# A two-direction state-space mixer with routed experts: one input multiply in three steps moved from GpSimd to VectorE

## The reference, cut to what matters

```
h = layernorm(x) * (1 + ca) + sa                  # x: 2 x 2048 tokens x 256
xn = layernorm(h, ln_w, ln_b)
# for each direction (forward, and on the reversed sequence), d = 0..511, n = 0..15:
xp, z = split(xn @ W_in.T)
xc = silu(causal_conv4(xp) + b_conv)
dt, B, C = split(xc @ W_x.T)
dt = softplus(dt @ W_dt.T + b_dt)
state[d, n] = state[d, n] * exp(dt[d] * A[d, n]) + (dt[d] * xc[d]) * B[n]   # token after token
y[d] = sum_n state[d, n] * C[n] + xc[d] * D[d]
out += 0.5 * (y * silu(z)) @ W_out.T
# then a layernorm, top-2 of 8 experts per token, and a shared expert
```

## Time and profile before

| | |
|---|---|
| median of 3 runs | 2154.33 us (2154.12 to 2154.85) |
| the profiled execution, its own time | 2153.5 us |
| its span in the trace | 2151.8 us |
| steps 1 to 15, from the start of step 1 to 1672 us | 1490 us |
| one step with states fed in | 98.3 to 100.5 us |
| granted clock of TensorE over the span (1 is 2.4 GHz) | 0.915 |

### The profile page before, as it was taken

The page is one execution under the profiler, slowest core; times in us unless marked ns, Lnnn a source line. Parts: engine busy times, 40 slices in busy tenths (PEclk is TensorE's granted clock), DMA queues, the critical chain, the costliest instruction groups (busy, mean ns, idle before and its releaser), DMA issues.

```text
span 2151.8 us, 26056 instructions
## 1 busy us (share of the span) xinstructions
PE 1872.8 (87%) x6376; PEld 794.9 (37%) x6377; DVE 1956.5 (91%) x1814; ACT 1523.8 (71%) x3148; POOL 1807.5 (84%) x624
## 2 busy tenths in 40 slices
PE   7889898988989898989898888889775799999997
PEld 3323232323333332323232323333221466655554
DVE  7989999999999999999999999999999776556776
ACT  5876879798888879786878888887956333434443
POOL 5689999999999999999999999999999333415444
PEclk9988898989889898989898998989876899999999
DMA  7746445353625354453535263545434652335444
GB/s 261 248 111 155 105 124 123 101 127 102 156 74 145 97 142 109 122 124 110 127 102 142 77 156 89 135 112 126 102 98 135 235 187 79 109 80 80 78 78 70
DMA packets 140347, 265.32 MB, mean 123 GB/s; under 512 B 21264, under 2 KB 44048, under 8 KB 139072
## 3 DMA queue, kind: packets, MB, share of 16 engines
q1 hardware_dynamic: 125488, 242.05, 41.7%
q0 software_dynamic: 13440, 17.93, 5.0%
q10 hardware_dynamic: 1296, 3.93, 0.5%
HBM read 194.51 MB, written 70.39 MB: 123 GB/s over the span
## 4 chain that ended last, share of the span: by engine, by line
POOL 28%; PE 26%; issue 16%; ACT 15%; DVE 10%; DVEq 2%; DMA 2%; POOLq 0%; SPq 0%; ACTq 0%
POOL hst L940 20%; POOL dbu L928 6%; ACT psum L1257 6%; DVE hst L1611 5%; PE psum L2188 5%; PE psum L2031 4%; PE psum L2200 3%; PE psum L2251 2%; POOL dt L920 2%; PE psum L1951 2%; PE psum L1979 2%; PE psum L1963 1%; DVE dbu L1590 1%; ACT dbu L1289 1%; PE psum L2271 1%
## 5 line engine op out<-in xcount | busy, mean ns | idle before, releaser
L940 POOL TENSOR_TENSOR hst<-hst,c_rep 128x2048 f32<-128x2048 f32 x254 | 1145.6, 4539 | 4.3 <-ACT state L1243 4.3
L1611 DVE TENSOR_TENSOR_SCAN hst<-psum,state,dbu 128x1024 f32<-128x1024 f32 x384 | 878.9, 2330 | 6.1 <-ACT psum L1257 5.5
L1257 ACT ACTIVATE psum<-dt_rep,neg_a 128x512 f32<-128x512 f32 (+1 forms) x1024 | 659.8, 676 | 135.1 <-DVE hst L1611 131.0
L1590 DVE TENSOR_TENSOR dbu<-psum,b_rep 128x2048 f32<-128x2048 f32 x176 | 398.7, 2265 | 8.4 <-PE psum L2016 8.0
L928 POOL TENSOR_TENSOR dbu<-dtu_rep,b_rep 128x2048 f32<-128x2048 f32 x80 | 363.9, 4549 | 8.3 <-DMA dtu_rep<-dtu_scratch 5.6
L2031 PE MATMUL psum<-hst,same 128*32 128x512 f32 x2048 | 285.1, 707 | 82.6 <-POOL hst L940 76.3
L1611 DVE TENSOR_TENSOR_SCAN hst<-psum,dbu 128x1024 f32<-128x1024 f32 x128 | 285.8, 2271 | 13.5 <-ACT psum L1257 12.9
L2016 PE MATMUL psum<-dt,same 32*128 32x512 f32 x352 | 215.6, 694 | 88.8 <-DVE dbu L1590 83.5
L1963 PE MATMUL psum<-xp,taps 128*128 128x512 f32 x512 | 236.6, 605 | 6.6 <-ACT sp_tmp L1226 6.5
L1050 POOL DMA_INDIRECT out_x<-h,target_u x72 | 112.3, 1560 | 153.0 <-DMA out_x<-h,target_u 78.4
L2031 PEld LDWEIGHTS psum<-hst,same 128*32 128x32 f32 x2048 | 68.2, 127 | 307.5 <-issue 172.0
(11 more groups left out here) (186 smaller groups left out, 2516.2 us busy)
## 6 DMA issues: line engine op xcount, KB each, us to landing
dt_rep<-dt_scratch SPq DMA_DIRECT2D x256, 256.0 KB, 4.8
dtu_rep<-dtu_scratch SPq DMA_DIRECT2D x320, 64.0 KB, 1.9
taps<-taps_scratch SPq DMA_DIRECT2D x64, 256.0 KB, 4.6
b_rep<-bc_scratch SPq DMA_DIRECT2D x64, 256.0 KB, 5.0
c_rep<-bc_scratch SPq DMA_DIRECT2D x64, 256.0 KB, 7.8
dt_scratch<-dt SPq DMA_DIRECT2D x63, 256.0 KB, 5.9
h<-slot_scratch SPq DMA_DIRECT2D x72, 129.5 KB
sp_tmp<-t_scratch SPq DMA_DIRECT2D x16, 512.0 KB, 7.0
```

The lines of the kernel that those rows point to most:

```text
L940: nc.gpsimd.tensor_tensor(h, h, c_rep[q % 2][:], ALU.mult).then_inc(prod_done, 1)
L1257: nc.scalar.activation(psum[:, PS_A + i, kept], dt_rep[:, G % 2, j, kept], ACT.Exp, scale=neg_a[:, q % 2, u, i:i + 1]).then_inc(exp_done, 1)
L1590: nc.vector.tensor_tensor(dbu[:, U % DBU, :, :], psum[:, PS_U:PS_U + 1, :].broadcast_to((P, NG, TB)), b_rep[U // UNITS % 2][:], ALU.mult). ...
L1611: nc.vector.tensor_tensor_scan(both(hst[:, U % RING, groups, :]), both(psum[:, PS_A + 2 * pair:PS_A + 2 * pair + 2, :]), both(dbu[:, U % D ...
```

## The change

It takes unit 7 of steps 1, 8 and 9 off GpSimd and gives it to VectorE. The functions that ask who multiplies a unit, or count the multiplies of each engine, follow from `on_pool`. SyncE no longer stores and reads back that unit's rows in these steps. TensorE gets one `spread_input(7)` more in each of them, put ahead of `sum_chunk` at T = 5.

```diff
+LIGHT_STEPS = (1, 8, 9)
...
 def on_pool(U):
-    return U % UNITS in POOL_UNITS
+    return U % UNITS in POOL_UNITS and (U // UNITS not in LIGHT_STEPS or U % UNITS != 7)
...
 def pool_mults(U):
-    return len(POOL_UNITS) * (U // UNITS) + sum(u <= U % UNITS for u in POOL_UNITS)
+    return sum(on_pool(u) for u in range(U + 1))
...
             for q in range(STEPS):
...
-                spread_dtu(q, 7)
+                if on_pool(UNITS * q + 7):
+                    spread_dtu(q, 7)
...
                 if t == 8 or (t == 13 and ahead) or T == 5:
                     spread_input(T + 3)
+                if q in LIGHT_STEPS and t == 5:
+                    spread_input(T + 2)
                 if T == 5:
                     project_dt(0, 3)
                 if t % GN == 1 and T > GN:
                     sum_chunk(T // GN - 1)
-                if 0 < T < ALL_UNITS - 2 and not on_pool(T + 2) and T != 6 and t != 9 and t != 14:
+                if 0 < T < ALL_UNITS - 2 and not on_pool(T + 2) and T != 6 and t not in (5, 9, 14):
                     spread_input(T + 2)
```

## The result

The changed kernel took **2161.03 us** in the median of 8 runs (2158.89 to 2164.21), the kernel before 2154.34 in the median of 8 beside it (2153.54 to 2155.5). The two medians differ by 6.7 us; the ratio on record is 1.0034 (7.3 us), with a 95% interval of 1.0025 to 1.0043: 5 to 9 us slower. The prediction said 2154.8 us and no difference; its range ended at 2159.0. The median misses the range by 2 us, and the kernel is slower where 0.77 of the chance was on "the same".

What follows compares the result with a forecast made beforehand. GpSimd's sum of work was taken as the bound; its shifts of +0.8, -0.8 and +0.5 us summed to +0.5 on an execution of 2153.5 us, 2154.0. With the median 0.8 above, the forecast was 2154.8 us, range 2151.0 to 2159.0.

Steps and rivals of the forecast that it cites:

- The bound: GpSimd's sum of work sets the mixer's end; time follows GpSimd's shift, as long as it doesn't go idle later on.
- What is taken away: Three GpSimd multiplies of 4.5 us, 13.5 us in all; the stores and loads that go with them cost nothing.
- What VectorE pays: Three added multiplies on VectorE, 2.2 us from start to start each, 6.6 us; GpSimd loses nothing by it.
- The new path: At unit 5, step 8: multiply of unit 6, spread, product, sum, z 1, copy, kept state, then GpSimd's weighing: 8.6 us.
- Weighing of unit 5 can start at M + 8.6: GpSimd's start on unit 5 in step 8, before at M + 9.4: 0.8 of 4.5 us kept, 3.7 us idle.
- M: End of VectorE's multiply of unit 6 in a light step, from which the new path is counted; 914.88 in step 8.
- it waits for VectorE's multiply: TensorE's added spread, 1.06 us per step, waits for the multiply of unit 6, with sum and z 1 queued behind.
- Step by step: GpSimd's shift after steps 1, 8 and 9: +0.8, 0.0 and +0.5 us; VectorE's waits give way.
- 13 us of new idle time on GpSimd and 0.5 us too late: What the forecast said becomes of the three steps' gain of 13.5 us.
- The slower one: Rival: the multiply for unit 10 becomes the new wait; about 2161 us if VectorE's waits don't give way; chance 0.15.
- the one on the port: Rival: the added VectorE multiplies block GpSimd, 2.2 us each and 7 in all: 2161 us; chance 0.02.
- The faster one: Rival: the kept state doesn't decide, GpSimd is held by the scan of unit 6 alone; about 2149 us; chance 0.11.

Runs made afterwards that it cites:

- vector_twice: Kernel before, with VectorE's multiply of unit 8 done twice in steps 1, 8 and 9 and nothing else: 2157.03 us, ratio 1.0007.
- fill2: Changed kernel plus two extra overwritten products with diag_d on TensorE ahead of the spread of unit 7 in the three steps: 2155.38 us, ratio 1.0001.
- product_z1_first: Changed kernel with the product with diag_d, then z 1, ahead of the spread of unit 7 on TensorE: 2149.43 us, ratio 0.9978 to the kernel before.
- wait_only: Kernel before, with TensorE waiting ahead of the sum for VectorE's multiply of unit 6 in steps 1, 8 and 9, nothing moved: 2158.34 us, ratio 1.0014.
- save_first: Changed kernel with the kept state of unit 5 ahead of the copy of z 1 on ScalarE in the three steps: 2160.59 us, ratio 1.0026.
- spread_after_sum: Changed kernel with the spread of unit 7 behind the sum and ahead of z 1 on TensorE: 2152.03 us, ratio 0.9991.
- step8_only: Changed kernel with the move in step 8 alone: 2156.88 us, ratio 1.0009 to the kernel before.
- z1_first: Changed kernel with z 1 alone projected ahead of the spread of unit 7 in the three steps: 2155.31 us, ratio 1.0001.
- product_first: Changed kernel with the product with diag_d alone ahead of the spread of unit 7 on TensorE: 2155.7 us, ratio 1.0005, runs 2153.29 to 2161.03.

## Why the prediction was wrong

**The bound: right.** The time follows GpSimd's work plus its idle time. Step 7 is unchanged, and between 175 and 1690 us the only idle times are the three that were named, ahead of the weighing of unit 5.

**What is taken away, 13.5 us: right.** No load became late: no wait of GpSimd for a DMA from 175 us on.

**What VectorE pays, 2.2 us per step: right**, and so was it that waits give way for it (in two of three steps of vector_twice). The multiplies took 2263 ns in the mean over all of after, as in the earlier trace rows. That the added work does not slow GpSimd is as predicted: GpSimd's weighings took 4548 ns in the mean against 4539.

**The new path: the mechanism right, the size wrong.** "Weighing of unit 5 can start at M + 8.6" is the step that failed. It starts at 930.89 with M = 919.39, M + 11.5, in step 8, and at M + 12.0 in step 1. The terms for the spread (1.06, measured 2.07), for the product (1.06, measured 2.01) and for the sum (3.57, measured 4.50) were mis-sized, 2.9 us together; the other terms are off by under 0.1. Each was read from the earlier trace rows, where the clock was 1.00 behind a wait of 1.68 us. The change itself makes another wait there. In the prediction "it waits for VectorE's multiply" is a place in the queue, never a length: from the end of the spread of unit 6 at about 912.6 and M = 914.88 its length would have come out at 2.3 us. With it the question would have been what TensorE does behind such a wait, and the trace of before had an answer, some 20 us further on in the same step. These are TensorE's timeline and its windows in the kernel before, at unit 9:

```profile
934.03 1.16 PE L2016 MATMUL psum<-dt,same 32*128 32x512 f32 x1 [3.81 <-DVE dbu L1590]
...
938.99 2.08 PE L2027 MATMUL psum<-xc,diag_d 128*128 128x512 f32 x2 [1.10 <-DVE sz L1583]
943.49 5.75 PE L2031 MATMUL psum<-hst,same 128*32 128x512 f32 x32 [2.42 <-POOL hst L940]
```
```profile
934.00:938.90 4.90, 3.85 (x6) 1.24 (x6) 4.90 (x4) 2.97 (x6) 4.90 (x2) 0.51 0.00 0
```

Here are the same product at 2.08 and the same sum at 5.75 us. They follow on a wait of 3.81 us for the same line and shorter ones of 1.10 and 2.42 us, and the clock is 0.51 in the first 5 us. The earlier trace rows had shown it from afar: a mean clock of 0.93 in a step that holds stretches at 1.00 must hold others at less. With these rows the three links would have had 5.7 us at one end (clock 1.00) and at the other, with two passes at some 2.1 and a sum of 5.75, 9.9 us: up to 4.2 us more per step, and a range that reaches beyond 2164 us. The Trainium skill has the rule on its page "TensorE: Matmul & The Clock Gate", section HAM oscillation — how this bites in real kernels: a gap in TensorE's work can bring the gate back to half the clock, and the work behind the gap then starts cold each time. The trace agrees here: 2.63 us of waiting in front, 0.50 of the clock and 2.07 us for 1.12 behind it. The page's example has longer gaps than most of those measured here.

**Step by step.** The prediction's shifts of GpSimd come out at +0.8, -0.8 and +0.5; measured are +2.5, +2.4 and +3.1. The clock alone explains nearly all of it in steps 8 and 9, where the weighing starts 2.9 us later behind M than predicted (M + 11.5 both times). In step 1 it is 3.4 us later, but GpSimd's distance to M was mis-sized as well: without the move it would have come to unit 5 at M + 9.4 in after (226.93 + 4.5, M = 222.01), while the prediction had M + 7.8 from the earlier trace rows. That 7.8 belonged to one execution: fill2, with the clock at 1.00 there, has 9.5, and this is why its wait in step 1 is 3.66 us.

**A sum that was wrong.** "13 us of new idle time on GpSimd and 0.5 us too late" can't both be: work gone of 13.5 us and a shift of +0.5 make 14.0 us of idle time. By the prediction's own terms the three waits are 5.3, 3.7 and 5.0 us, and not 3 to 4 each as its last paragraph says. This does not touch the time that it forecast.

**The rivals.** The slower one got the sign and, by chance, the time (2161 us, as did the one on the port), but not the cause: in after GpSimd's multiplies wait for nothing (the row of L931 above), and VectorE's waits do give way. The faster one, that the kept state is not what decides, is refuted in after; its time of about 2149 us is what product_z1_first reached, by making the chain through z 1 shorter. VectorE gains next to nothing there, as predicted (at most 0.3 us per step): its first scans of steps 8, 9 and 10 come only 0.1 to 0.2 us earlier than before. The gain is GpSimd's alone, 1.7 us in step 8 and 0.6 in step 9.

**The forecast's spread.** All of its uncertainty was in signals of 0.1 us and in waits that give way. The one large unknown, how fast a matmul runs behind a new wait, had a single value.

## What to carry to other kernels

A wait that an edit puts into TensorE's queue can have two prices: its length, and that of the matmuls right behind it at half the clock. Work out its length, then look in the trace of before for waits as long and read what the same instructions took behind them, and carry both values to the ends of the range. An operation that is queued before its operand is ready makes everything behind it wait; give it a place behind work that is ready, as the product and z 1 were here. And when work is taken from the engine that bounds the kernel, what counts is when the next gate opens: the gain is the work gone less the idle time that comes, and it can be negative. A distance between two engines that is read from one execution, such as the M + 7.8 here, can be another in the next.

## What was not expected of the hardware

The granted clock behind waits of about the same length came out both ways. It was 0.50 to 0.61 after 2.38, 2.63 and 3.56 us in after, 1.00 after 2.38 us in step 1 of wait_only, and low after 2.38 us in its step 8. In step 8 of save_first the spread and the product behind a wait of 2.38 us took 1.12 us each, and the sum that began 2.1 us later took 5.33. After waits of 1.67 to 1.71 us the sum took 3.64 us in before, in spread_after_sum and in two steps of vector_twice, but 5.33 after 1.65 us in its third and 5.13 after 1.72 in step8_only; z 1 took 1.98 us after 1.70 in z1_first and 3.54 after 1.57 in product_z1_first. What decides between them stays open: no run here varies the wait finely enough. It can also be why product_first, one program, ran between 2153 and 2161 us; that was not shown, since only one of its runs has a trace.
